# Order of the four projections of a head pair, and the shape of the row-sum products, in a two-attention transformer stack

## What is computed

```python
def attn_a(x, kernel, WO):                      # 16 heads of 64, 4 sequences of 1024
    q = einsum('bsm,hmd->bhsd', x, kernel[0]); k = ...kernel[1]; v = ...kernel[2]
    attn = softmax(einsum('bhsd,bhtd->bhst', q, k) * scale)
    return einsum('bhst,bhtd->bhsd', attn, v) ... @ WO
def attn_b(x, ...):
    h = layernorm(x) * ln_scale + ln_bias
    q = rope(up_q(down_q(h))); k = rope(up_k(down_kv(h))); v = up_v(down_kv(h))
    return softmax(q k^T / 8) v ... @ w_out.T + x
x = x + attn_a(norm(x)); x = x + ffn(norm(x)); x = x + attn_b(norm(x)); x = x + ffn(norm(x))
```

## Time and profile before

| | us |
|---|---|
| median of 3 executions | 3870.42 (3868.67 to 3873.36) |
| the profiled execution | 3868.46 |
| its span, first to last instruction | 3866.7 |
| outside the span | 1.8 |
| features_a | 0 to about 65 |
| attention a | about 65 to 1770 |
| first feed-forward layer | to about 2030 |
| attention b | to about 3662 |
| second feed-forward layer | to the end |

### The profile page before, as it was taken

The page is one execution under the profiler, slowest core; times in us unless marked ns, Lnnn a source line. Parts: engine busy times, 40 slices in busy tenths (PEclk is TensorE's granted clock), DMA queues, the critical chain, the costliest instruction groups (busy, mean ns, idle before and its releaser), DMA issues. The chain is left out here.

```text
span 3866.7 us, 60118 instructions
## 1 busy us (share of the span) xinstructions
PE 3650.3 (94%) x16736; PEld 2354.9 (61%) x16736; DVE 2262.3 (59%) x2988; ACT 1689.1 (44%) x3212; POOL 2624.3 (68%) x1467
## 2 busy tenths in 40 slices
PE   3999999999999999997975999999999999999799
PEld 2566666666666666656863555555555555555488
DVE  5444444444444444445756777777777767777354
ACT  1344444444444444444542444444444444444354
POOL 2677777778777777773323777887788778777521
PEclk9999999999999999998996999999999999999899
DMA  6334433343344434421114455445544454554100
GB/s 194 81 80 88 103 78 75 84 109 84 81 85 87 95 75 86 87 47 32 44 62 90 80 86 103 83 84 86 103 83 84 83 105 82 85 83 83 40 17 28
DMA packets 419601, 313.68 MB, mean 81 GB/s; under 512 B 254753, under 2 KB 292513, under 8 KB 418465
## 3 DMA queue, kind: packets, MB, share of 16 engines
q1 hardware_dynamic: 414400, 291.48, 38.2%
q10 hardware_dynamic: 5088, 20.97, 1.5%
HBM read 88.35 MB, written 21.50 MB: 28 GB/s over the span
## 5 line engine op out<-in xcount | busy, mean ns | idle before, releaser
L887 POOL TENSOR_TENSOR a_rs<-a_rs,a_p 128x1024 f32<-128x1024 f32 x384 | 916.0, 2385 | 317.9 <-ACT a_p L797 301.0
L814 DVE TENSOR_REDUCE a_nmax<-a_ps_x 128x1 fp32r<-128x1024 f32 x512 | 627.2, 1225 | 759.4 <-PE a_ps_x L620 755.8
L887 POOL TENSOR_TENSOR b_rs<-b_rs,b_p 128x1024 f32<-128x1024 f32 x384 | 916.8, 2387 | 227.0 <-ACT b_p L797 208.9
L814 DVE TENSOR_REDUCE b_nmax<-b_ps_x 128x1 fp32r<-128x1024 f32 x512 | 626.7, 1224 | 326.5 <-PE b_ps_x L620 322.3
L797 ACT ACTIVATE a_p<-a_ps_s 128x512 f32<-128x512 f32 x1024 | 529.7, 607 | 413.6 <-PE a_ps_s L636 412.8
L797 ACT ACTIVATE b_p<-b_ps_s 128x512 f32<-128x512 f32 x1024 | 530.6, 608 | 340.6 <-PE b_ps_s L636 332.0
L652 PE MATMUL a_ps_o<-a_p,a_v 128*64 128x512 f32 x2048 | 467.7, 598 | 0.0
L652 PE MATMUL b_ps_o<-b_p,b_v 128*64 128x512 f32 x2048 | 467.7, 598 | 0.0
L635 PE MATMUL b_ps_s<-b_q,b_k 128*128 128x512 f32 x1024 | 419.5, 410 | 2.9 <-ACT b_p L797 1.5
L635 PE MATMUL a_ps_s<-a_q,a_k 128*128 128x512 f32 x1024 | 416.2, 406 | 3.0 <-DMA a_q<-a_nmax 3.0
L636 PE MATMUL b_ps_s<-b_q,b_k 128*128 128x512 f32 x1024 | 404.7, 395 | 0.0
(11 more groups left out here) (166 smaller groups left out, 5692.8 us busy)
## 6 DMA issues: line engine op xcount, KB each, us to landing
a_k<-a_nat_h SPq DMA_DIRECT2D x256, 128.0 KB, 2.4
a_q<-a_nat_h SPq DMA_DIRECT2D x256, 128.0 KB, 2.4
b_k<-b_nat_h SPq DMA_DIRECT2D x256, 128.0 KB, 3.9
b_q<-b_nat_h SPq DMA_DIRECT2D x256, 128.0 KB, 3.8
a_k<-a_nat_l SPq DMA_DIRECT2D x128, 128.0 KB, 2.4
a_q<-a_nat_l SPq DMA_DIRECT2D x128, 128.0 KB, 2.4
a_rinv<-rows_a SPq DMA_DIRECT2D x128, 128.0 KB, 3.0
b_k<-b_nat_l SPq DMA_DIRECT2D x128, 128.0 KB, 4.0
```

The costliest lines, as they stand in the source:

```text
L814: dve.reduce_max(nmax[:, g % 2, head, qi:qi + 1], ps_x[:].rearrange("p a b -> p (a b)"), AX_X, negate=True).then_inc(s_red, 1)
L887: pool.tensor_tensor(out, out, p[:, bb, i, :], ALU.add).then_inc(s_sum, 1)
```

## The change

The four units of a pair are projected in the order q half 0, k half 0, k half 1, q half 1 (`which_half`). The places of `nat_h` and `nat_l` still go by the parity of `n`; the rounded q weights get two buffers, by the parity of the pair. The semaphores of the stacks, the loads of q and k weights and the two splits follow the new order. SyncE stacks one unit at the start of every window and one at its end, where odd windows had both at the end. `row_sums` makes four products of 32 columns of ones by 256 columns of `rs`, one for each strip of 32 PSUM partitions, instead of two of 64 by 512. So the sums fill 256 columns of PSUM in place of 512, `rb` is copied at that width, and `sums_to_tile` takes two DMAs a head instead of one. The core of the diff:

```diff
-        wq_r, wq_h, wq_l = sb("wq_r", [P, WC]), sb("wq_h", [P, WC], F32R), sb("wq_l", [P, WC], F32R)
+        wq_r, wq_h, wq_l = sb("wq_r", [P, WC]), sb("wq_h", [P, 2, WC], F32R), sb("wq_l", [P, 2, WC], F32R)
-        ones = sb("ones", [P, D])
+        ones = sb("ones", [P, P // 4])
-        rb, rinv = sb("rb", [P, BLOCK]), sb("rinv", [P, BLOCK])
+        rb, rinv = sb("rb", [P, E]), sb("rinv", [P, BLOCK])
+        def which_half(n):
+            return ((1, 0), (0, 0), (0, 1), (1, 1))[n % 4]
...
-            for head in range(2):
-                pe.matmul(ps_t[D * head:D * (head + 1), 1, :], ones[:], rs[:, g % 2, head * BLOCK:(head + 1) * BLOCK],
-                          start=True, stop=True).then_inc(s_r, 1)
+            for i in range(4):
+                pe.matmul(ps_t[32 * i:32 * (i + 1), 1, 0:E], ones[:], rs[:, g % 2, i * E:(i + 1) * E],
+                          start=True, stop=True, tile_position=(0, 32 * i)).then_inc(s_r, 1)
...
             if n % 4 == 0:
                 pe.wait_ge(s_feat, due(t, 16, 16 * (pair // 2 + 1)))
+                pe.wait_ge(s_wq, due(t, 4, 2 * (pair + 1)))
+            if n % 4 == 1:
                 pe.wait_ge(s_wk, due(t, 4, 2 * (pair + 1)))
-            if n % 4 == 2:
-                pe.wait_ge(s_wq, due(t, 4, 2 * (pair + 1)))
...
-                    act.activation(rb[:], ps_t[:, 1, :], ACT.Copy).then_inc(s_rb, 1)
+                    act.activation(rb[:], ps_t[:, 1, 0:E], ACT.Copy).then_inc(s_rb, 1)
...
-                    split(pool, t, wk_r, wk_h, wk_l, s_wkr, s_unit, due(t, 8, 4 * pair - 2), s_wk, pair, 2)
+                    split(pool, t, wq_r, wq_h[:, pair % 2, :], wq_l[:, pair % 2, :], s_wqr, s_unit,
+                          due(t, 8, 4 * pair - 4), s_wq, pair, 2)
...
-                    split(pool, t, wq_r, wq_h, wq_l, s_wqr, s_unit, due(t, 8, 4 * pair), s_wq, pair, 2)
+                    split(pool, t, wk_r, wk_h[:], wk_l[:], s_wkr, s_unit, due(t, 8, 4 * pair - 1), s_wk, pair, 2)
...
-            sp.dma_start(rq[:, head, :], rb[D * head:D * head + 1, :].rearrange("o (p a) -> o p a", a=BT)
-                         ).then_inc(s_rq, 16)
+            for half in range(2):
+                row = D * head + 32 * half
+                sp.dma_start(rq[D * half:D * (half + 1), head, :],
+                             rb[row:row + 1, :].rearrange("o (p a) -> o p a", a=BT)).then_inc(s_rq, 16)
...
-            if u % 2 == 0 and live(t, 8, n, 4 * NPAIR):
+            if live(t, 8, n, 4 * NPAIR):
                 sp.wait_ge(s_nat_l, due(t, 8, n + 1))
                 stack(sp, n)
...
-            if u % 2 == 1 and live(t, 8, n, 4 * NPAIR):
-                stack(sp, n)
+            if u % 2 == 1 and live(t, 8, n + 1, 4 * NPAIR):
                 stack(sp, n + 1)
```

More of the change, by code:

```diff
@@ L615, in maxima @@
                     for half in range(2):
-                        pe.wait_ge(s_stack[half], due(t, 2 * SD, SD * (pair + 1)))
-                pe.wait_ge(s_stack[2 + g % 2], due(t, 2 * SD, SD * (pair + 1)))
+                        pe.wait_ge(s_stack[1 + half], due(t, 2 * SD, SD * (pair + 1)))
+                pe.wait_ge(s_stack[3 * (g % 2)], due(t, 2 * SD, SD * (pair + 1)))
             pe.wait_ge(s_red, due(t, 32, c))
@@ L684, in project_qk @@
         def project_qk(pe, t, u, n):
-            pair, which, half = n // 4, (n % 4) // 2, n % 2
+            pair = n // 4
+            which, half = which_half(n)
             if n % 4 == 0:
                 pe.wait_ge(s_feat, due(t, 16, 16 * (pair // 2 + 1)))
+                pe.wait_ge(s_wq, due(t, 4, 2 * (pair + 1)))
+            if n % 4 == 1:
                 pe.wait_ge(s_wk, due(t, 4, 2 * (pair + 1)))
-            if n % 4 == 2:
-                pe.wait_ge(s_wq, due(t, 4, 2 * (pair + 1)))
             pe.wait_ge(s_nat_l, due(t, 8, n))
-            w_h, w_l = (wk_h, wk_l) if which == 0 else (wq_h, wq_l)
+            w_h, w_l = (wk_h, wk_l) if which == 0 else (wq_h[:, pair % 2, :], wq_l[:, pair % 2, :])
             if rope is not None:
@@ L750, in convert_hi @@
         def convert_hi(act, t, n):
-            half, which = n % 2, (n % 4) // 2
+            half, which = n % 2, which_half(n)[0]
             if rope is None:
@@ L817, in rotate_odd @@
         def rotate_odd(dve, t, n):
-            cols = slice((n % 2) * BLOCK, (n % 2 + 1) * BLOCK)
+            half = which_half(n)[1]
+            cols = slice(half * BLOCK, (half + 1) * BLOCK)
             dve.wait_ge(s_unit, due(t, 8, n + 1))
@@ L853, in dve_window @@
                 if b == 0 and live(t, 4, u - 2, NGROUP):
-                    dve.wait_ge(s_rq, due(t, 128, 32 * (u - 1)))
+                    dve.wait_ge(s_rq, due(t, 256, 64 * (u - 1)))
                     dve.wait_ge(s_row, due(t, 128, 32 * (u - 2)))
@@ L870, in split @@
             pool.wait_ge(s_used, used)
-            pool_round(pool, hi[:], raw[:], zero).then_inc(s_split, 1)
+            pool_round(pool, hi, raw[:], zero).then_inc(s_split, 1)
             pool.wait_ge(s_split, due(t, 2 * per_body, 2 * pair + 1))
-            pool.tensor_tensor(lo[:], raw[:], hi[:].bitcast(F32), ALU.subtract).then_inc(s_split, 1)
+            pool.tensor_tensor(lo, raw[:], hi.bitcast(F32), ALU.subtract).then_inc(s_split, 1)
         def pool_window(pool, t, u):
@@ L907, in stack @@
         def stack(sp, n):
-            pair, which, half = n // 4, (n % 4) // 2, n % 2
+            pair = n // 4
+            which, half = which_half(n)
             for head in range(2):
                 rows = slice(D * head, D * (head + 1)) if rope is None else slice(head, P, 2)
-                hi, lo = nat_h[rows, half, :].bitcast(F32), nat_l[rows, half, :].bitcast(F32)
+                hi, lo = nat_h[rows, n % 2, :].bitcast(F32), nat_l[rows, n % 2, :].bitcast(F32)
                 if which == 0:
@@ L956, in sp_window @@
             if u % 2 == 1 and live(t, 2, (u + 5) // 2, NPAIR):
-                sp.wait_ge(s_wq, due(t, 4, u + 5))
+                sp.wait_ge(s_wk, due(t, 4, u + 5))
             if live(t, 4, u - 2, NGROUP):
@@ L967, in sp_window @@
                 source = source_of(t, 3 + u // 2)
-                sp.wait_ge(s_wk, due(t, 4, u + 6))
-                sp.dma_start(wk_r[:], w_qk[source, :, WC:2 * WC]).then_inc(s_wkr, 16)
+                sp.wait_ge(s_wq, due(t, 4, u + 6))
+                sp.dma_start(wq_r[:], w_qk[source, :, 0:WC]).then_inc(s_wqr, 16)
             if u == 2 and live(t, 1, 2, BODIES):
```

16 lines of the change are left out of this document (8 added, 8 removed).

## The result

| | us |
|---|---|
| median of 4 executions, changed kernel | 3816.41 (3814.50 to 3817.55) |
| the kernel before on the same chip, 4 executions | 3870.43 (3868.67 to 3873.36) |
| ratio | 0.9861, 95% interval 0.9849 to 0.9873 |
| span of the profiled execution | 3814.2, before 3866.7 |

The change saves 54 us, 1.4%. The forecast was 3834, with a gain of 36.5 in its sum, and the range 3814 to 3861 holds the result, 2.4 us above its lower end; the band of the likeliest case, 3820 to 3848, does not. I first read TensorE, then the row-sum block, then the places where TensorE waits.

The account below looks back on a forecast made before the run. TensorE, busy 94% of the span, was taken as the bound. From 3868.46 us, 33.5 for row sums and 4.8 at starts came off, 1.8 at ends was added: 3832.0, plus 2.0 to the median, 3834.0; range 3814 to 3861.

Parts of the forecast that it names:

- the likeliest case: Whole kernel: gain of 0.17 to 0.36 us a window, 0 to 7 us at the starts, 3820 to 3848 us; chance 0.60.
- the row sums: Between `values` and the next maxima: cost falls from 0.86 to 0.59 us, 0.27 us in each of 124 windows, 33.5 us.
- the rival in which the change of width is free: Going to 32 columns behind `values` costs nothing: gain 0.41 us a window, 50.8 us, 3817 us; chance 0.10.
- two strips at a time: Row-sum products run only in pairs: four rounds, 0.86 us as before, plus 0.16 us a window, 3887 us; chance 0.13.
- the 644 ns of the earlier trace: First record at the new width lasts 644 ns where others last 592, read as another 0.05 us for the width change.
- Copy, sums to tile, reciprocal: Behind the row sums: two more DMAs delay the reciprocal some tenths of a us at most, which disappears behind `values`; 0.
- In even windows SyncE is free 3.8 us earlier; nothing on the path gets this: SyncE's queue in even windows: `to_row` no longer waits behind twelve stack issues, with no gain in time.
- The rival of the stacks in front of `spread`: Odd windows of b: output exceeds its 6.2 us cover by 1.6 us, 50 us lost, about 3883 us; chance 0.05.
- Starts: Start of each stage: first unit's stack issued earlier, first maxima 2.5 us sooner in a, 2.3 in b, 4.8 in all.
- Sequence changes: Where b changes sequence: the output wait, 1.60 us in one of three, sits behind the feature load, which does not move; 0.
- Ends of the stages: Last group's way over `rq`: two more issues, 1.18 us less 0.3, so 0.9 us lost a stage, 1.8 for both.
- In b the gain is taken by VectorE: Reduction behind the row sums in b has 0.24 us of slack, so only a gains: 3851 us; chance 0.12.

Follow-up runs that it names:

- the width alone: The kernel before with two row-sum products of 32 columns by 512 instead of 64 by 512, records and DMAs unchanged: 3883.81 us, ratio 1.0040.
- four DMAs alone: The kernel before, wide row-sum products kept, each head's row sent to `rq` in two pieces, so four DMAs a window instead of two: 3910.33 us, ratio 1.0106.
- order alone: The changed kernel with two wide products, the full copy and two DMAs to `rq` as before, one stack still moved to the window's start: 3846.44 us, ratio 0.9944.
- order with late stacks: Projections q, k, k, q with wide sums and two DMAs, but both stacks of odd windows issued at the window's end: 3870.04 us, ratio 1.0002.
- the one with two DMAs: The changed kernel with one DMA a head to `rq` (two source rows, 32 partitions apart), products still narrow: 3810.44 us, ratio 0.9846.
- the spread first: The changed kernel with SyncE issuing `spread` ahead of the window's first stack instead of behind it: 3822.11 us, ratio 0.9884.

## Why the prediction was right, and where its steps were not

The forecast of the largest term, the row sums, was right for its reason. That the range held the total was in part luck. The likeliest case by itself ended at 3820; the range reached down to 3814 for the rival in which the change of width is free, and that rival is refuted. The 16 us by which the profiled execution gained more than the sum said come from the sequence changes (9.6), the starts (2.9), the ends (2.6) and the rest (0.7).

**Row sums: right, in size and mechanism.** 0.59 us was forecast, 0.57 measured; four strips side by side, two rounds. Of its terms, the change of width (0.14 and 0.02 for the later start) is 0.12 in the kernel with that alone, and the second four start 0.24 us after the first, where 0.215 was taken. The rivals of two strips at a time and of a free change of width fall with this. By the efficiency that the Trainium skill gives for three column tiles (TensorE: Matmul & The Clock Gate, Measured speedup vs the span model) the eight records would take an estimate of 0.54 us, and the block 0.66 with the 0.12 added; the trace has 0.57 for the whole block, and the measurement decides. The Trainium skill (TensorEngine Tiling (Array Packing), Key Properties) says that changing the tiling mode drains TensorE; that the change costs time is borne out by the 0.12 us, the draining itself no run shows. One reading was misplaced: the 644 ns of the earlier trace rows are those of the last row sums of each stage alone. The records that last longer behind a change of width are the first of `values` (643 ns against 592), and in the kernel with the width alone the first row sums (617).

**"Copy, sums to tile, reciprocal": 0 was nearly right for this change and wrong as a step.** I followed the two additional DMAs to the reciprocal, and took a wait of some tenths of a us that disappears. In most windows there is none, but in four windows of b it is 0.7 to 1.3 us and does not disappear: it costs 3.9 us, by the rotation, which I had named, and by the conversion and the exponentials behind it, which I had not. What I did not ask at all was who stands behind them in SyncE's queue: twelve stack issues, whose landing ScalarE's conversion awaits, with the exponentials behind it. With the queue of before this costs 42 us (four DMAs alone). It cost no more than about 4 us here because the same change takes six of these twelve issues away. So "the sums" and "the order" were costed as two sums, and they are one.

**"In even windows SyncE is free 3.8 us earlier; nothing on the path gets this": wrong.** This is the true gain of the reordering. With wide sums the moved stack brings 21 us (order alone against order with late stacks), and in it are the starts and the sequence changes; with four DMAs it brings 70. The trace of before had the sign: the conversion at line 757 waited for the stack's DMA in every second window of b, 3.5 to 3.8 us. I passed it over since TensorE showed no wait. In the changed kernel this wait is gone from all windows, and the 21 us need the new order only in that it frees the place which the early stack writes. The rival of the stacks in front of `spread` did not come true: in steady windows TensorE waits nowhere for `b_o`.

**Starts: right mechanism, too small.** 2.7 and 4.2 us to the first maxima, where I took 2.5 and 2.3. With late stacks the kernel has neither (22.2 and 31.7 us to the first maxima, as before), so it is the stack's early issue, as forecast. In b, I took only the conversion's own wait.

**Sequence changes: 0 forecast, 9.6 measured.** I wrote that the wait sits behind the load of the features, which does not move. The load does not; what is issued just ahead of it does. Before, `to_row` stood behind twelve stack issues and the next stack, of q, went out at 2391.19, 2.1 us ahead of the load, so its last two DMAs fell behind the load and landed 10.5 and 10.6 us after their issue, and the maxima waited for them. After, it is a stack of k that goes out 2.8 us ahead, and one DMA of it falls behind. The maxima's wait, which was 1.3 to 1.7 us, and the half clock are gone. The wait for `b_o` is left at 1.7 us, since the spread is still issued 1.0 us behind the load, and one for `b_nmax` of 0.7 to 1.6 us has come up. I also misread the size: the wait for the output was not 1.60 us in one of three but 1.60, 2.51 and 2.46 us, one in each. That half the load removes most of the rest, and that another order in the queue brings a wait of the maxima back, bears this out. In a the change gives 1.2 us here; where the stack alone was moved it gave 3.2.

**Ends of the stages.** I took a loss of 1.8 us for two DMAs on the last group's way, and there was a gain of 0.8. From the last row sums to the last output projection the kernel before takes 17.85 us in a and 18.01 in b, the changed kernel 16.89 and 18.21, and the one with two DMAs 16.88 and 16.36. So in b the two DMAs cost 1.9 us, in a nothing, by one execution each; what shortens these ends otherwise was not tested.

**In b the gain is taken by VectorE: no.** In b 0.29 us arrive in the median window. But the sentence of this rival that the change of order can do harm on VectorE or ScalarE was the nearest to the 42 us; it named no chain and no price, and put the harm on the order and not on the DMAs.

What stays open is why the reciprocal is late in just four steady windows of b, and why a's sequence changes grow with narrow sums and late stacks (by 7.4 us with two DMAs, by 11 and 13 with four).

## What to carry to other kernels

An in-order DMA queue is an engine of its own: price an added issue by who stands behind it, down to the compute engine that awaits the landing, and not only by who awaits the added transfer. A wait that costs nothing now (an engine off the path that waits in every window for the same DMA) tells where the slack is used up. And two edits of one change may be measured apart with opposite signs and still belong together; test them as a grid, not one by one. Near a bulk load, put the transfers that are needed soon ahead of it, or cut the load to what its first reader needs. And look at which place a transfer writes before you look for its place in the queue: a reordering that is worth nothing by itself can be what allows the early issue.

## What the runs showed of the hardware

- Four products of 32 columns on the four strips of the array start within some 20 ns of each other, and 256-column float32 records so follow in fours, 0.24 us apart. The block of eight takes 0.57 us with the change of width in it, that of four records of twice the length took 0.86.
- Going from 64 to 32 columns behind `values` costs 0.12 us each time, with the same number of records.
- Two more DMAs of 1 KB in a queue cost 1.27 us of issue time (2.45 against 1.18), and with twelve issues behind them they made a kernel of 3870 us 42 us slower.
- A DMA that was issued behind a 2 MB load on another queue landed only about when the load did, a large one like a small one: 128 KB in 9.3 us instead of 3.3, 0.5 KB in 8.7 (the median of eight, of which the last two were issued late) instead of 2.0, and in 5.0 behind a load of 1 MB. Five DMAs of 128 KB that were issued 0.4 to 2.8 us ahead of the load landed in 2.8 to 3.5 us.
- Behind waits of 1.33 and 1.60 us, 3 us apart, TensorE's granted clock was 0.50 (1.2 GHz); behind waits of 1.74 and 0.67 us at the same place it stayed at 1.00. At b's three sequence changes it fell in all three before and in none after; with the spread first it fell behind a single wait of 3.06 us.
